# Two expert heads: one filling stage shortened, lane comparisons in four operations, one product for row numbers, an exponential moved ahead

## The reference

```
logits = x @ gate_w                    # 2048 tokens, 8 experts
w, idx = top_k(softmax(logits), 2)     # layer 3 divides w by its sum
h      = gelu(x @ w1[e]) @ w2[e]       # first layer: 512 hidden
h      = (silu(x @ w1[e]) * (x @ w3[e])) @ w2[e]   # second: 256 hidden
t      = t + sum over the 2 chosen experts of w * h
```

## Time and profile before

| | |
|---|---|
| median of 3 runs | 636.5 us (633.36 to 638.74) |
| the profiled execution | 634.37 us, of which the span of the profile is 632.6 us |
| mean granted clock of PE | 0.766 |
| busy: PE, DVE, POOL, ACT | 516.1, 437.6, 286.4, 272.2 us |

### The profile page before, as it was taken

How to read it: one execution, slowest core, us unless ns; L and a number is a source line. 1 busy time by engine, 2 the same in 40 slices (tenths; PEclk the granted TensorE clock), 3 DMA queues, 4 the chain that set the end, 5 groups by cost and what they waited for, 6 DMA issues and landing times. The chain is left out here.

```text
span 632.6 us, 10638 instructions
## 1 busy us (share of the span) xinstructions
PE 516.1 (82%) x3070; PEld 402.1 (64%) x3070; DVE 437.6 (69%) x1314; ACT 272.2 (43%) x722; POOL 286.4 (45%) x272
## 2 busy tenths in 40 slices
PE   9998985989568999999158899999856788877742
PEld 4785563859535999998157777777636345555531
DVE  2628569998784457444488799999997855555535
ACT  4523143300312754444016999999942023333311
POOL 1093447978244677774212111111111157777740
PEclk9698586989677999999655555555555789999985
DMA  6000060000721111121400000000004011112216
GB/s 222 1 1 2 0 266 0 1 2 0 248 85 34 43 51 50 56 52 34 144 3 0 2 2 0 0 0 0 1 2 133 2 36 52 51 51 55 49 58 177
DMA packets 26511, 31.09 MB, mean 49 GB/s; under 512 B 3106, under 2 KB 21539, under 8 KB 26339
## 3 DMA queue, kind: packets, MB, share of 16 engines
q1 hardware_dynamic: 21474, 20.29, 9.9%
q0 software_dynamic: 4992, 10.23, 6.2%
HBM read 20.16 MB, written 10.36 MB: 48 GB/s over the span
## 5 line engine op out<-in xcount | busy, mean ns | idle before, releaser
L1091 POOL DMA_INDIRECT rows_out<-yo,idy x78 | 77.8, 997 | 39.2 <-DVE yo L1457 20.6
L1085 POOL DMA_INDIRECT xg<-rows_in,idx x78 | 75.6, 969 | 37.2 <-issue 21.6
L1147 ACT ACTIVATE hraw<-ps 128x512 f32<-128x512 f32 (+1 forms) x78 | 38.3, 491 | 107.4 <-PE ps L1253 107.4
L1449 DVE TENSOR_TENSOR hidden<-ps,hidden 128x512 fp32r<-128x512 f32 (+1 forms) x78 | 43.3, 555 | 45.9 <-ACT hidden L1154 45.9
L1274 PE MATMUL ps<-wHL,hidden 128*128 x234 | 69.0, 346 | 6.7 <-issue 3.9
L1277 PE MATMUL ps<-wHL,hidden 128*128 x234 | 54.0, 231 | 0.0
L1274 PEld LDWEIGHTS ps<-wHL,hidden 128*128 128x128 f32 x234 | 44.0, 188 | 15.5 <-issue 15.3
L1605 ACT ACTIVATE p<-s 128x256 bf16<-128x256 bf16 x128 | 51.6, 413 | 3.3 <-DVE s L1797 3.3
L1565 POOL CAST vp<-v3f 128x256 bf16<-128x256 f32 x8 | 3.5, 439 | 95.2 <-ACT s L1596 95.2
L1251 PE MATMUL ps<-wHL,xa 128*128 x78 | 34.8, 447 | 14.1 <-issue 12.2
L1444 DVE TENSOR_TENSOR hraw<-hraw,ps 128x256 f32<-128x256 f32 x39 | 16.4, 421 | 41.1 <-ACT hraw L1147 41.1
(11 more groups left out here) (286 smaller groups left out, 1390.0 us busy)
## 6 DMA issues: line engine op xcount, KB each, us to landing
wraw<-in_ex SPq DMA_DIRECT2D x2, 2048.0 KB, 9.9
rows_in<-both SPq DMA_DIRECT2D x8, 512.0 KB, 6.1
both<-rows_out SPq DMA_DIRECT2D x16, 256.0 KB, 4.1
wraw<-in_ex SPq DMA_DIRECT2D x1, 3072.0 KB, 12.3
w<-in_pack SPq DMA_DIRECT2D x1, 1582.0 KB, 8.2
xg<-rows_in,idx POOLq DMA_INDIRECT x78, 2.6
rows_out<-yo,idy POOLq DMA_INDIRECT x78, 2.3
xs<-in_x SPq DMA_DIRECT2D x4, 256.0 KB, 4.6
```

The source lines that it names most:

```text
L1085: pool.indirect_dma_start(xg[:, j % NXG, :], None, xs_d[:], bass.IndirectOffsetOnAxis(idx[:, j:j + 1], 0)).then_inc(ld[j % NXG], 16)
L1091: pool.indirect_dma_start(ys_d[:], bass.IndirectOffsetOnAxis(idy[:, j:j + 1], 0), yo[:, j % NYO, :], None).then_inc(st[j % NYO], 16)
L1147: act.activation(hraw[:, j % 2, :], ps[:, HB + j % 2, 0:hid], ACT.Gelu if layer == 0 else ACT.Silu).then_inc(z["act"], 1)
L1449: dve.tensor_tensor(hL[:, j % 2, :], ps[:, HTB + j % 2, 0:hid], hH[:, j % 2, :].bitcast(F32), ALU.subtract).then_inc(z["hL"], 1)
```

## The change

Five edits, all in `experts`.

1. `FILL2` is 3 instead of 5.
2. The 32 comparisons for `lanes`, each of 128 elements with a number per partition, become four of 1024 elements with two tensor inputs; `lane_of` is bf16, and repeated along the place. The counter `one` is raised after each of the four as it was after each eighth.
3. In layer 1 POOL made its part of `rowno` in four operations; now it is one in both layers.
4. For that the slots of layer 1 are written in another order, by two reductions into `pos` instead of one.
5. ACT's exponential of the first half stands ahead of its two copies of transposed rows in layer 0, and between the second and the third of its four in layer 1.

```
-            ... lane_of = ... own(f"lane_of_{layer}", [P, R * TOPK])
+            ... lane_of = ... own(f"lane_of_{layer}", [P, R * TOPK], BF16)
-            MB, FILL, FILL1, FILL2 = 1, 3, 7, 5
+            MB, FILL, FILL1, FILL2 = 1, 3, 7, 3
+            def exponential(act, g):
+
+                act.wait_ge(z["ep"], z0["ep"] + g + 1)
+                act.activation(pg[:, GR * g:GR * (g + 1), :], lg[:, GR * g:GR * (g + 1), :], ACT.Exp).then_inc(z["e"], 1)
...
-                if layer == 0:
-                    x = pool.tensor_tensor(rowno[:, :, 1], hits[:], wc("iota", 0, R * TOPK)[:, :, None].to_broadcast([P, R * TOPK, NT]), ALU.mult)
-                else:
-                    for n in range(TOPK * S):
-                        of = slice(n // S * R + n % S, (n // S + 1) * R, S)
-                        x = pool.tensor_tensor(rowno[:, of, 1], hits[:, of], wc("iota", n * B, (n + 1) * B)[:, :, None].to_broadcast([P, B, NT]), ALU.mult)
+                x = pool.tensor_tensor(rowno[:, :, 1], hits[:], wc("iota", 0, R * TOPK)[:, :, None].to_broadcast([P, R * TOPK, NT]), ALU.mult)
...
+                    exponential(act, 0)
                     for g in range(2):
                         act.wait_ge(gs["ltp"], 2 + g)
...
                     for c in range(NCH):
+                        if c == 2:
+                            exponential(act, 0)
                         act.wait_ge(c4["tp"], c + 1)
...
-                for g in range(2):
-                    act.wait_ge(z["ep"], z0["ep"] + g + 1)
-                    act.activation(pg[...], lg[...], ACT.Exp).then_inc(z["e"], 1)
+                exponential(act, 1)
...
-                        chained(dve.tensor_reduce(pos[:].rearrange("p k r -> p r k"), sel[:], AX.X, ALU.add))
+                        for n in range(1 if layer == 0 else S):
+                            of = slice(0, R) if layer == 0 else slice(n, R, S)
+                            at = slice(0, R) if layer == 0 else slice(n * B, (n + 1) * B)
+                            x = dve.tensor_reduce(pos[:, :, at].rearrange("p k r -> p r k"), sel[:, of], AX.X, ALU.add)
+                        chained(x)
...
-                    for i in range(RK):
-                        x = dve.tensor_scalar(lanes[:, i], iotab[:], lane_of[:, i:i + 1], None, ALU.is_equal)
-                        if i % (RK // CHK) == RK // CHK - 1:
-                            x.then_inc(z["one"], 1)
+                    for q in range(CHK):
+                        some = slice(q * RK // CHK, (q + 1) * RK // CHK)
+                        dve.tensor_tensor(lanes[:, some], lane_of[:, some, None].to_broadcast([P, RK // CHK, P]),
+                                          iotab[:][:, None].to_broadcast([P, RK // CHK, P]), ALU.is_equal).then_inc(z["one"], 1)
```

More of the change, by code:

```diff
@@ L1000, in experts @@
             parts = own(f"parts_{layer}", [P, 2, R * TOPK], I32)
-            tile_of, lane_of = own(f"tile_of_{layer}", [P, R * TOPK], BF16), own(f"lane_of_{layer}", [P, R * TOPK])
+            tile_of, lane_of = own(f"tile_of_{layer}", [P, R * TOPK], BF16), own(f"lane_of_{layer}", [P, R * TOPK], BF16)
             wtmp = own("wtmp", [P, P]) if layer == 0 else None
@@ L1124, in _ @@
                     for c in range(NCH):
+                        if c == 2:
+                            exponential(act, 0)
                         act.wait_ge(c4["tp"], c + 1)
                         act.activation(pair_columns(c), pair_bank(c, c4), ACT.Copy).then_inc(z["lt"], 1)
-                for g in range(2):
-                    act.wait_ge(z["ep"], z0["ep"] + g + 1)
-                    act.activation(pg[:, GR * g:GR * (g + 1), :], lg[:, GR * g:GR * (g + 1), :], ACT.Exp).then_inc(z["e"], 1)
+                exponential(act, 1)
                 if layer == 0:
```

## The result

The changed kernel takes 629.57 us, median of 13 runs (628.74 to 632.96). Beside it the kernel before took 634.07 us, also 13 runs (633.33 to 638.74). The ratio is 0.9928, 95% interval 0.9907 to 0.9949: 4.5 us less, with an interval of about 3.2 to 5.9 us. In the profiled executions the span falls from 632.6 us to 627.4, 5.2 us.

What follows compares the result with a forecast made beforehand. No engine bounds a head; a chain of waits across PE, ACT and DVE does, ending in the filling products. 0.5 + 0.45 - 0.1 + 0.57 + 0.5 + 1.2 + 1.7 = 4.8 us off the 636.5 median: 631.7, range 628.0 to 637.0.

Steps and rivals of the forecast that it cites:

- Exponentials first: Both heads: ACT's first-half exponential ahead of its copies lets DVE's second centring come earlier, gaining 0.5 and 0.45 us.
- The cover: Both heads: waiting for PE's second logits hides most of the exponential's gain; without it 1.8 and 1.5 us would come.
- Slots' numbers in two operations: Second head only: one more small DVE operation on the path, costing 0 to 0.2 us, taken as 0.1.
- Lanes: Both heads: four single-rate operations held up by POOL, 1.14 us each after the first's 1.09; gain 0.57 and 0.5 us.
- rival 3: Lanes at double rate: 2.35 us behind POOL instead of 4.51, 2.15 more gained per head, 627.4 us; chance 0.06.
- one product of 2.56 us ends at 500.31: Second head: POOL's single product replaces four running 497.75 to 500.70; part of the lanes' gain of 0.3 to 0.7 us.
- Filling: Behind the map: three calls instead of five bring the first expert product earlier, by 1.2 and 1.7 us in the heads.
- What is late next is thus the gather: Before the first expert product: with three calls PE waits for the second gather's landing, at 198.2 and 511.5, not the filling.
- lower bound: Filling gain of 1.0 and 1.5 us, if a full microsecond lies between the gather's landing and the first expert product.
- Rival 4: The loop doesn't follow: its end is set by gathers tied to the map, 2.9 us don't come, 634.6; chance 0.09.
- Rival 1: PE's clock rise is missed before the loop: up to 2.3 us per head, 634.0 or in both 636.3; chance 0.35.
- Rival 2: Slower: PE's clock low for 6.8 us in both loops, costing 3.4 us each, 638.5 us; chance 0.05.

Runs made afterwards that it cites:

- pool_only: Kernel before, with POOL's row numbers in one product in the second head and the slots written by two reductions: 634.68 us, 0.9999.
- lanes4_only: Kernel before, with the lanes in four two-tensor operations and lane_of in bf16; POOL's four products stay: 631.82 us, 0.9966.
- fill1: Changed kernel with one call of filling products behind the map instead of three: 631.95 us, 0.9961 of the kernel before.
- fill3_only: Kernel before, with three filling calls behind the map instead of five, nothing else: 631.52 us, 0.9963.
- fill5_back: Changed kernel with five filling calls behind the map again: 631.44 us, 0.9958 of the kernel before.
- dve_rowno: Changed kernel with POOL's product of the row numbers made by DVE, ahead of its own part: 628.32 us, 0.9922 of the kernel before.
- steady: Changed kernel with five filling calls and a 256-column filling product behind each of the map's first three quarters: 629.26 us, 0.9924 of the kernel before.

## Why the prediction was right

The median came out at 629.57 us, inside 628.0 to 637.0, and 2.1 us under the forecast of 631.7. The sum said 4.8 us less; the medians give 4.5 and the spans 5.2. The 2.1 us are thus not in the sum but in what it was set on: the median of three runs was 636.5, that of 13 is 634.07, 2.4 less. The prediction had given such a median "some 2 us of its own". Set on the profiled execution, as the working did first, it was 629.6 against 629.24. The range alone proves little, since it also holds the 634.07 of the kernel before. What bears out the working is that its terms were found one by one: 0.51 + 0.49 - 0.06 + 0.60 + 0.57 + 1.18 + 1.81 = 5.1 us, where the span fell by 5.2.

**Exponentials first.** 0.5 and 0.45 us forecast; centring to centring (start of L1316 and L1314, of L1317 and L1315 after) is 6.06 and 5.71 us before, 5.55 and 5.22 after: 0.51 and 0.49. The cover was the one named, PE's logits, and the copy behind the exponential in the second head was not pushed by anything that shows.

**Slots' numbers in two operations.** 0.1 us forecast; the two reductions take 0.48 us where one took 0.42: 0.06.

**Lanes.** 0.57 and 0.5 us forecast; hits to the lanes' end is 9.25 and 9.26 us before, 8.65 and 8.69 after: 0.60 and 0.57. The single rate is shown: 1212 ns for 1024 elements, beside 1458 for the 1248 of hits. So rival 3 falls, and the earlier trace rows, the form that repeats an element, was the right neighbour to take the price from, not the earlier trace rows. The Trainium skill reports a close case on another page than the one weighed ("Vector Engine (DVE) Microarchitecture Reference", 5.1 Performance modes): with one element read 16 times as an input, a two-source operation of 2-byte operands ran at single rate. The 1212 ns, for one element read 128 times, agree.

**One reason was wrong.** For the second head the prediction counted POOL's single product as part of the gain ("one product of 2.56 us ends at 500.31"). The row after shows DVE behind POOL, the worse of the two cases, and its price was right: the lanes end 502.37 - 497.49 = 4.88 us after POOL's product, 4.51 and 0.37 more. What the prediction had wrong is POOL's 2.56 us, taken from the first head. There DVE's 0.55 us operation ran unhindered and POOL's had to wait for it; in the second head POOL's went first and took 2.27. So the two orders cost the same, and the gain is 0.57. pool_only shows that the single product brings nothing by itself, and lanes4_only that 0.58 comes without it. The taken 0.5 us came true because the lanes alone bring it; that part is luck.

**Filling.** 1.2 and 1.7 us forecast; 1.18 and 1.81 measured. "What is late next is thus the gather": the wait at 197.22 names it, and fill1, which ends its filling 3 us earlier, gains nothing on the first product. From the second transposition's start to the first product it is 0.85 and 0.76 us, near the "full microsecond" of the lower bound. The second head's 6.20 us lie a little under the 6.3 to 6.7 that were to be seen. The working however took the clock of before as given, and counted all six records as slow although it has the clock rise after 4.6 us, which makes 5.0 us and not 5.4. Neither matters for the first product: fill3_only, with the low clock of before, has it after 6.54 and 6.53 us. But in the changed kernel the low stretch is half as long, and there five calls may have cost less than the forecast's 6.8 us; what two calls are worth behind the other edits stayed open (fill5_back). The 1.18 and 1.81 us are thus the gain from filling to product, and not shown to be all the work of this one edit.

**The loop follows.** Rival 4 falls: the first scatter of the second loop is 4.9 us earlier and the end 5.2, and POOL's wait ahead of it shrank from 2.84 to 1.01 us, by what PE gained there.

**The clock.** Rival 1 described a real mechanism that the changed kernel's profiled execution didn't meet: its clock is at 1.00 when the loop begins. With one call it happens, for 6.7 us per loop, at 2.2 and 1.5 us. dve_rowno and steady show that three or five calls can meet it too in one loop, at 1.15 and 1.1 us for 3.3 us of low clock. So whether other executions of the changed kernel met it is not known. Rival 2, the low stretch of 6.8 us in both loops, is what fill1 shows, but not at its price: 3.7 us were lost there in the two loops together and not 6.8, and fill1 is still faster than before.

## What to carry to other kernels

Filling products that keep PE's clock up are worth their time only until what the next stage waits for has landed. Find that landing (here the second gather's) and count the filling in microseconds, not in calls: ten records took 4.5 us at the high clock and up to 7.2 at the low one. Ending it 1.5 to 1.7 us ahead of the second gather cost nothing in the changed kernel's profile; cutting it further left PE idle for 3.3 and 2.2 us, and 2.2 and 1.5 us were lost in the loops. Where POOL and DVE hold each other up as in these rows, count one sum for both, and try each step on the engine that does it faster. And weigh edits together: those that shorten the same slow stretch need not add up.

## What the runs showed of the hardware beyond what was expected

**POOL and DVE take turns by whole instructions.** A 0.55 us DVE operation took 2.66 us beside POOL's 2.27 us product, and four of each became 6.17 and 4.92 us instead of 4.62 and 2.95. The Trainium skill ("GPSIMD Engine Reference", 1. Specifications) names contention of POOL with DVE instructions that read two SBUF inputs or run in a two-port mode; the trace agrees, and adds that POOL's work in four pieces or in one makes no difference (0.9999).

**Some of the spread between runs is in the first 30 us.** The changed kernel had 3 of 13 runs at 632.7 to 633.0 us, some 3.5 us above the rest. fill5_back's profiled execution is such a late one, and shows a place: the attention products of the first encoder stage (one line's instructions, ns min/median/max) in the changed kernel

```profile
L319 PE MATMUL ps<-k,q x32: 374/374/629, 15.0 to 23.5; 16*128 16x256 f32 x32
```

and in fill5_back, where that code is the same:

```profile
L319 PE MATMUL ps<-k,q x32: 374/626/626, 15.6 to 26.7; 16*128 16x256 f32 x32
```

Windows of the same two executions, the changed kernel first:

```profile
16.00:20.00 4.00, 4.00 (x20) 3.44 (x19) 2.44 (x2) 1.68 (x7) 0.00 (x0) 1.00 0.00 0
```

```profile
16.00:20.00 4.00, 4.00 (x16) 3.23 (x15) 1.58 (x2) 1.16 (x5) 0.00 (x0) 0.73 0.00 0
```

The clock fell some 2 us earlier, more of the 32 products ran at 1.2 GHz, and they took 11.79 us instead of 9.07. Everything after them is later by about that. In the other ten profiled executions the 32 products took 9.1 to 10.0 us. Whether the changed kernel's three late runs have this cause is not shown, since they left no trace. A clock that falls in both loops, at 3.7 us in fill1, would make as much, and it is Rival 1 again.
